# Causal attention on one core: value products two steps behind the scores and across the end of a round, copies and transposes spread over steps, masks of 128 columns

## What is computed

```python
Q = (X @ Wq.T + bq).reshape(B, S, H, d_head) * scale      # B 4, S 1024, H 16, d_head 16
K = (X @ Wk.T + bk).reshape(B, S, H, d_head) * scale
V = (X @ Wv.T + bv).reshape(B, S, H, d_head)
scores = jnp.einsum('bqhd,bkhd->bhqk', Q, K)
scores = jnp.where(causal[None, None], scores, -jnp.inf)
attn = jax.nn.softmax(scores, axis=-1)
out = jnp.einsum('bhqk,bkhd->bqhd', attn, V).reshape(B, S, D)
```

## Time and profile before

| | |
|---|---|
| median of 3 runs | 2040.08 (2039.08 to 2040.45) |
| profiled execution | 2036.14 |
| its span | 2034.0 |
| TensorE busy in the span | 1682.5 (83%) |
| VectorE, ScalarE, GpSimd busy | 1383.6, 939.3, 672.0 |
| the 15 round periods, by the first score of each | 858.34 to 1379.25 |
| last round | 1379.25 to about 1410 |

### The profile page before, as it was taken

The page is one execution under the profiler, slowest core; times in us unless marked ns, Lnnn a source line. Parts: engine busy times, 40 slices in busy tenths (PEclk is TensorE's granted clock), DMA queues, the critical chain, the costliest instruction groups (busy, mean ns, idle before and its releaser), DMA issues. The chain is left out here.

```text
span 2034.0 us, 35680 instructions
## 1 busy us (share of the span) xinstructions
PE 1682.5 (83%) x10296; PEld 1295.6 (64%) x10296; DVE 1383.6 (68%) x2825; ACT 939.3 (46%) x2201; POOL 672.0 (33%) x850
## 2 busy tenths in 40 slices
PE   2899985709991780799999999996789999979997
PEld 2787774509991560455555555542579999968886
DVE  5688887506665876977777777760467777646776
ACT  0456562304443651066666666664444444433343
POOL 1555530750007824043434334343000000047760
PEclk9799998959995995899999999998899999989999
DMA  6445523723434996333535354422774444466661
GB/s 217 181 141 168 156 47 65 230 91 117 125 113 127 332 355 190 85 105 86 147 85 144 94 129 109 118 68 64 205 216 125 125 126 125 127 212 182 202 181 47
DMA packets 288529, 293.13 MB, mean 144 GB/s; under 512 B 122665, under 2 KB 245034, under 8 KB 286300
## 3 DMA queue, kind: packets, MB, share of 16 engines
q1 hardware_dynamic: 265340, 236.62, 39.6%
q0 software_dynamic: 18432, 50.36, 7.9%
q10 hardware_dynamic: 4608, 4.20, 0.6%
HBM read 144.97 MB, written 141.82 MB: 141 GB/s over the span
## 5 line engine op out<-in xcount | busy, mean ns | idle before, releaser
L1705 ACT ACTIVATE ca_PT<-ca_psS 128x512 f32<-128x512 f32 (+3 forms) x768 | 344.9, 493 | 272.8 <-PE ca_psS L1740 260.4
L1631 DVE TENSOR_REDUCE ca_part<-ca_psM 128x1 f32<-128x512 f32 (+3 forms) x608 | 368.6, 657 | 85.3 <-PE ca_psM L1725 60.5
L1740 PE MATMUL ca_psS<-ca_QS,ca_KS 128*128 128x512 f32 (+3 forms) x768 | 305.7, 408 | 4.2 <-ACT ca_PT L1705 4.1
L1033 POOL DMA_INDIRECT g_y<-ys_scratch,pos x128 | 129.6, 1013 | 441.7 <-POOLq L68 395.0
L1718 PE MATMUL ca_psM<-ca_KS,ca_QS 126*128 126x512 f32 (+3 forms) x768 | 246.5, 364 | 15.6 <-issue 12.8
L1740 PEld LDWEIGHTS ca_psS<-ca_QS,ca_KS 128*128 128x128 f32 x768 | 147.1, 194 | 106.7 <-ACT ca_PT L1705 101.7
L1718 PEld LDWEIGHTS ca_psM<-ca_KS,ca_QS 126*128 126x128 f32 x768 | 141.1, 193 | 37.9 <-DVE ca_part L1631 15.6
L1752 PE MATMUL ca_psO<-ca_PT,ca_VA 128*32 128x512 f32 (+3 forms) x1536 | 160.7, 497 | 1.3 <-POOL ca_PT L1611 1.3
L1609 POOL TENSOR_TENSOR ca_waited<-ca_waited 1x1 f32<-1x1 f32 x128 | 23.4, 183 | 341.7 <-ACT ca_PT L1705 341.7
L626 POOL DMA_INDIRECT xs_scratch<-x_sb,pos x128 | 123.3, 964 | 36.8 <-issue 36.8
L497 PE MATMUL fa_psO<-fa_weighed,ident 128*128 128x256 f32 x512 | 124.0, 398 | 8.1 <-DVE fa_weighed L356 8.0
(11 more groups left out here) (288 smaller groups left out, 4567.2 us busy)
## 6 DMA issues: line engine op xcount, KB each, us to landing
f_xs<-xs_scratch SPq DMA_DIRECT2D x214, 128.0 KB, 2.1
ys_scratch<-f_ys SPq DMA_DIRECT2D x214, 128.0 KB, 1.7
xs_scratch<-fa_blank SPq DMA_DIRECT2D x32, 640.0 KB, 4.1
ca_QS<-qk_scratch SPq DMA_DIRECT2D x32, 512.0 KB, 6.6
ca_KS<-qk_scratch SPq DMA_DIRECT2D x32, 512.0 KB, 8.2
xs_scratch<-fa_blank SPq DMA_DIRECT2D x32, 384.0 KB, 3.4
f_raw<-in_ffn SPq DMA_DIRECT2D x16, 608.0 KB, 4.0
v_scratch<-gp_v_st SPq DMA_DIRECT2D x32, 256.0 KB, 4.5
```

What stands on the lines that cost most here:

```text
L1033: pool.indirect_dma_start(dst[:, k, :], None, y_dram, bass.IndirectOffsetOnAxis(pos[:, tile, k:k + 1], 0)).then_inc(got, 16)
L1631: dve.tensor_reduce(dst, psM[(slot * NU + u) % SLOTS][:, 0:nh * w].rearrange("p (h k) -> p h k", h=nh), AX.X, ALU.max)\
L1705: act.activation(PT[:, s % 2, h, off:CHUNK], psS[(GH * s + h) % SLOTS][:, off:CHUNK], ACT.Exp)\
L1740: pe.matmul(psS[tile % SLOTS][:, off:CHUNK], KS[:, slot, h, kt * P:(kt + 1) * P], QS[:, slot, h, c * CHUNK + off:(c + 1) * CHUNK], start=T ...
```

## The change

- `LAG` = 2: the block of step s−2 is issued at the end of step s, and this goes on over the end of a round: blocks 10 and 11 of a round stand in steps 0 and 1 of the next.
- `PT` has three buffers (`PTS`).
- `COPY`, `TURN`, `USE`: copy, transposes and division stand in steps 6, 9, 10 for c = 0, and in steps 2, 3, 4 of the next round for c = 1. On VectorE copy and division come behind the step's first unit.
- The transpose of the maxima is issued in step 7, one step behind `whole`, and the negation is split off (`negate`) into step 8.
- The mask matmul covers 128 columns a head.
- `pull` waits for the scores of the round before for Q and K and for its blocks for V; it stands ahead of the output, and the maxima rows stand ahead of the output of c = 0.
- The rows of ones are loaded in pieces of 128 elements. The rounds are written as one plain loop.

```diff
-    SLOTS = 3
+    SLOTS, PTS, LAG = 3, 3, 2
-        PT = sb("PT", [P, 2, GH, CHUNK])
+        PT = sb("PT", [P, PTS, GH, CHUNK])
-        one_rows = sb("one_rows", [2, CHUNK])
+        one_rows = sb("one_rows", [2, P])
-        ORDER = "0u1u2u3uv"
+        COPY, TURN, USE = (WHOLE - 1, 2), (WHOLE + 2, 3), (WHOLE + 3, 4)
...
-                if not (isinstance(n, int) and n < SLOTS):
-                    sp.wait_ge(oT_done, (n - SLOTS + 1) * SPAN)
+                if n >= SLOTS:
+                    sp.wait_ge(s_done, (n - SLOTS + 1) * (GH * NS))
...
+                if n >= SLOTS:
+                    sp.wait_ge(pv_done, (n - SLOTS + 1) * NS)
+                sp.dma_start(VA[:, slot, :, :], v_dram[n].rearrange("t p c -> p t c")).then_inc(stack_in[slot], 16)
...
+            for n in range(ROUNDS):
+                if n + SLOTS - 1 < ROUNDS:
+                    pull(n + SLOTS - 1)
+                if n:
+                    output(n - 1, 1)
+                if n + 1 < ROUNDS:
+                    maxima_rows(n + 1, (n + 1) % SLOTS)
                 output(n, 0)
...
         @block.vector
+            def step(n, s):
+                todo = [(n + 1 + s // WHOLE, u) for u in ahead[s] if n + 1 + s // WHOLE < ROUNDS]
+                for k in todo[:1]:
+                    unit(*k)
+                if s == COPY[1] and n:
+                    collect(n - 1, 1)
+                if s == USE[1] and n:
+                    divide(n - 1, 1)
+                if s == COPY[0]:
+                    collect(n, 0)
+                if s == USE[0]:
+                    divide(n, 0)
+                if s == WHOLE + 1 and n + 1 < ROUNDS:
+                    negate(n + 1)
+                for k in todo[1:]:
+                    unit(*k)
+                if s == WHOLE - 1 and n + 1 < ROUNDS:
+                    whole(n + 1)
...
         @block.scalar
-                    if s >= 2 or not first(n):
-                        act.wait_ge(pv_done, n * NS + s - 1)
+                    if n * NS + s >= PTS:
+                        act.wait_ge(pv_done, n * NS + s - (PTS - 1))
...
         @block.tensor
-                    m = min(w, 2 * P)
-                    mask = mask_qk[:, 2 * P - m:2 * P].unsqueeze(1).broadcast_to([P, nh, m])
-                    ins = pe.matmul(bank[:, 0:nh * w].rearrange("p (h k) -> p h k", h=nh)[:, :, w - m:w], ident_b[:, :], mask,
+                    mask = mask_qk[:, P:2 * P].unsqueeze(1).broadcast_to([P, nh, P])
+                    ins = pe.matmul(bank[:, 0:nh * w].rearrange("p (h k) -> p h k", h=nh)[:, :, w - P:w], ident_b[:, :], mask,
...
+            def step(n, s):
+                todo = [(n + 1 + s // WHOLE, u) for u in ahead[s] if n + 1 + s // WHOLE < ROUNDS]
+                for h in range(GH):
+                    scores(n, s, h)
+                    if h < len(todo):
+                        unit(*todo[h])
+                for k in todo[GH:]:
+                    unit(*k)
+                if s == TURN[1] and n:
+                    transpose_out(n - 1, 1)
+                if s == TURN[0]:
+                    transpose_out(n, 0)
+                if s == WHOLE and n + 1 < ROUNDS:
+                    transpose_maxima(n + 1)
+                if n * NS + s >= LAG:
+                    values(*divmod(n * NS + s - LAG, NS))
```

More of the change, by code:

```diff
@@ L1524, in causal_attention, with pull @@
         masked, slots_done = routing((ctx, block), PT[:, :, :, :].rearrange("p a h n -> p (a h n)"), psX)
[L1526 to L1537, removed]
         @block.sync
         def _(sp):
-            def pull(n, slot):
-                at = sp.snap(n) if not isinstance(n, int) else n
-                if not (isinstance(n, int) and n < SLOTS):
-                    sp.wait_ge(oT_done, (n - SLOTS + 1) * SPAN)
-                rows = qk_dram[:, :, bass.ds(at, 1), :, :].rearrange("c s a (r h) n -> s r c (a h n)", h=GH)
+            def pull(n):
+                slot = n % SLOTS
+                if n >= SLOTS:
+                    sp.wait_ge(s_done, (n - SLOTS + 1) * (GH * NS))
+                rows = qk_dram[:, :, n, :, :].rearrange("c s (r h) n -> s r c (h n)", h=GH)
                 for half in range(2):
@@ L1569, in _ @@
                 if n < SLOTS - 1:
[L1570 removed]
+                    pull(n)
                 if n == 0:
                     sp.wait_ge(filled, 2)
[L1573 to L1574 removed]
+                sp.dma_start(KS[STACK:P, n, :, :].rearrange("r h (c n) -> r (h c) n", n=P).bitcast(F32),
+                             one_rows[:, :].unsqueeze(1).broadcast_to([2, GH * POS_TILES, P])).then_inc(ones_done, 16)
             maxima_rows(0, 0)
[L1577 to L1582, removed]
[L1583 to L1588 removed]
+            for n in range(ROUNDS):
[5 more added lines that the diff above has]
+                    maxima_rows(n + 1, (n + 1) % SLOTS)
+                output(n, 0)
+            output(ROUNDS - 1, 1)
             for c in range(SPAN):
[L1590 removed]
                 sp.wait_ge(ao_stored[c], 16 * ROUNDS)
@@ L1636, in whole @@
                 lower, upper = part[:, 0, :, :], part[:, 1, :, TPC:]
-                if not first(n):
+                if n:
                     dve.wait_ge(mT_done, n)
@@ L1666, in divide @@
                                   ALU.mult).then_inc(o_out, 1)
-            def both(n, slot, turn, two_ahead):
-                for s in range(NS):
[L1670 to L1695, removed]
+            def step(n, s):
[16 more added lines that the diff above has]
+                    whole(n + 1)
+            for u in range(NU):
+                unit(0, u)
+            whole(0)
+            negate(0)
+            for u in range(FIRST):
+                unit(1, u)
+            for n in range(ROUNDS):
+                for s in range(NS):
+                    step(n, s)
+            collect(ROUNDS - 1, 1)
+            divide(ROUNDS - 1, 1)
         @block.scalar
@@ L1748, in values @@
                     pe.wait_ge(exp_done, n * (GH * NS) + GH * s + GH)
-                if kt == 0 and not (first(n) and c == 0):
+                if kt == 0 and (n or c):
                     pe.wait_ge(ot_out, n * SPAN + c)
@@ L1817, in _ @@
             pe.wait_ge(masked, 2)
             pe.wait_ge(ones_done, 16 * SLOTS)
-            rounds(pe, both, front, back)
+            pe.wait_ge(stack_in[0], 16 * LOADS)
+            for u in range(NU):
+                unit(0, u)
+            transpose_maxima(0)
+            pe.wait_ge(stack_in[1], 16 * LOADS)
+            for u in range(FIRST):
+                unit(1, u)
+            for n in range(ROUNDS):
+                pe.wait_ge(m_in[n % SLOTS], (n // SLOTS + 1) * 16)
+                for s in range(NS):
+                    if s == WHOLE and n + 2 < ROUNDS:
+                        pe.wait_ge(stack_in[(n + 2) % SLOTS], ((n + 2) // SLOTS + 1) * (16 * LOADS))
+                    step(n, s)
@@ L1822, in project_out @@
+            for s in range(NS - LAG, NS):
+                values(ROUNDS - 1, s)
+            transpose_out(ROUNDS - 1, 1)
 def project_out(nc, tag, o_tile, keep, s_dram, ident, wo_dram, bo_dram, scale, E, w_dram, w_hi, w_lo, shared=None):
```

120 lines of the change are left out of this document (38 added, 82 removed).

## The result

The changed kernel takes 2028.51 us (median of 6 runs, 2017.21 to 2032.23) beside 2040.07 for the kernel before (6 runs, 2034.74 to 2043.34). The ratio is 0.9938 with a 95% interval of 0.9910 to 0.9967: faster, by 7 to 18 us. Forecast was 2024, with a range of 2010 to 2034 (and a narrower one of the author's own, 2018 to 2030).

The account below looks back on a forecast made before the run. TensorE was taken to set the pace. Terms −1.29 + 0.46 + 0.62 − 0.69 = −0.90 us a round, with the end rounds −16.3 in all, gave 2024 us; range 2010 to 2034, own range 2018 to 2030.

Parts of the forecast that it names:

- the masks: Mask matmuls, 22 a round: narrower ones save 0.69 us a round, 0.10 for each of four going from 512 to 256.
- the new wait: Step 2: block 0 waits for VectorE's accumulator copy, queued behind that step's first unit; adds 0.62 us a round.
- one removed wait: Transpose of the maxima: its wait for VectorE's last maximum goes when issued one step later; −0.23 us a round.
- The removed waits: Waits at the round's end, before the maxima's transpose and at the round's start go; together −1.29 us a round.
- The end of the round: TensorE's wait for the accumulator copy before the transposes goes, with a block-to-transpose change; −0.89 us a round.
- step 0 runs into no exp: Start of the round: block 10 now stands in step 0, so ScalarE gets its time; −0.17 us a round.
- The rival of half price: Masks of 128 columns cost half, saving 0.05 each; 9.6 us more gain, 2014 us; chance 0.12.
- The separation: Blocks 10 and 11 become two blocks between scores, with one more entry and more returns; adds 0.46 us a round.
- The rounds at both ends: Round 0 gains 3.3 us, lacking earlier blocks, transposes and wait; rounds 14 and 15 together gain 1.3.
- Costed at nothing: Third value-product buffer, GpSimd's cut, SyncE's pulls, maxima rows, rows of ones and work before the first score: no cost.

Follow-up runs that it names:

- the run with 256 columns: The changed kernel with masks of up to 256 columns a head again, the new schedule kept: 2036.58 us in one run, period 34.68.
- the run with masks alone: The kernel before with masks of 128 columns and nothing else changed: 2027.86 us in one run, period 34.51.
- The pairs: The changed kernel with value blocks s-2 and s-1 together behind even steps, copies at steps 5 and 1: 2176.27 us (kernel before 2235.40); period 32.57 on a first-kind chip.
- with VectorE out of the way: The changed kernel with paired blocks, VectorE's copies and divisions first in their steps, units spread anew: 1993.28 us beside 2037.97, ratio 0.9787, period 31.8.
- the kernel with the copy first: The changed kernel with step 2's accumulator copy ahead of the step's first unit: 2018.13 us in one run, before 2040.81; period 33.50.
- the joined blocks: The changed kernel with blocks 10 and 11 together behind the next round's step 0, copy in step 1: 2172.59 us in one run, kernel before 2235.40.

## Why the prediction was right, and where its terms were off

**The stage.** Forecast −16.3, measured −12.7; the period 34.0, measured 34.23. The mechanism came as forecast, with the masks 0.24 a round too large, the new wait 0.10 too small and one removed wait 0.12 too small, so that the last two nearly cancel; that they do is luck. The median of the whole program (2028.5 against 2024) shows less than the stage does, since the stages ahead of it alone differ by 9.0 between the two profiles.

**The removed waits (−1.29)** held, and one of them was larger. The end of the round shows no idle, the maxima's transpose waits for nothing (1126.22, its block at 1126.42), and step 0 runs into no exp. But the earlier trace rows are of round 7, and round 7 is the exception for the maxima. There block 4 came 0.44 behind its score in step 5, and the transpose then waited 0.17. In the other middle rounds block 4 comes 0.32 behind, and the transpose waits 0.28. TensorE's timeline of the kernel before, steps 5 and 6 of round 8, and its waits from 858 to 1343 us:

```profile
1150.38 0.39 PE L1740 MATMUL ca_psS<-ca_QS,ca_KS 128*128 128x512 f32 x1
1150.70 1.07 PE L1752 MATMUL ca_psO<-ca_PT,ca_VA 128*32 128x512 f32 x8
...
1154.66 1.07 PE L1752 MATMUL ca_psO<-ca_PT,ca_VA 128*32 128x512 f32 x8
1156.00 0.29 PE L1733 MATMUL ca_psX<-ident,ca_maxima 128*32 128x128 f32 x1 [0.28 <-DVE ca_maxima L1641]
```

```profile
PE ca_psX L1767 <- DVE ca_OT L1656: 10.6, 13, 0.8
PE ca_psX L1733 <- DVE ca_maxima L1641: 3.6, 13, 0.3
```

Block to transpose is 1.34 there, against 1.23 in round 7 and 1.00 without a wait. So the term was −0.35 and not −0.23, another −0.12. One round read as typical was wrong by a tenth of a microsecond although the periods agree to 0.02.

**The new wait (+0.62)** was +0.72: it stands where it was placed, at the predicted instant (copy 1.27 into the step), but TensorE began 0.14 after the copy's end, and I had allowed 0.05. Moving the copy shows that the copy's place is the whole price of that wait, and that it could have been had for nothing.

**The masks (−0.69)** are the mis-sized term: −0.45 by the run with 256 columns, −0.41 by the run with masks alone. The four that went from 512 to 256 gave their 0.10 each and the one in front of a block its 0.05. The other fifteen gave nothing; I had given them 0.014 each, and two of 512 columns were left. The rival of half price is refuted by three runs: 0.45 where it wanted 1.3, 0.41 for the masks alone, and 2.66 without masks where it wanted 2.0. What holds a mask at 0.12 was not tried apart from its width; that it is the next instruction's weights stays my reading.

**The separation (+0.46)** fits the sum: −1.29 − 0.12 + 0.46 + 0.72 − 0.45 = −0.68, and 34.91 became 34.23. It is not measured apart from the removed waits; the run with 256 columns fixes only the two together. The pairs test the price of a block from the other side: six blocks fewer at 0.27 and no wait forecast 31.9, and with VectorE out of the way 31.8 came, 1.67 under the kernel with the copy first, or 0.28 a block. Loops written out, the place of the loads and the rows of ones were not tried alone; the sum leaves no room for them in a middle round.

**The rounds at both ends.** Rounds 1 to 13 gave 8.8 (forecast 11.7), the last two 1.5 (1.3). Round 0 took 32.42 instead of 34.83, 2.4 less where 3.3 was forecast. Of the missing 0.9 the period's own miss is 0.2. The rest is that without blocks in steps 0 and 1 its units outrun VectorE. TensorE's timeline in step 2 of round 0, then the weight loads of its two units:

```profile
871.62 0.50 PE L1708 MATMUL ca_psM<-ca_KS,ca_QS 126*128 126x512 f32 x1
871.96 0.28 PE L1727 MATMUL ca_psS<-ca_QS,ca_KS 128*128 128x256 f32 x1
872.22 0.50 PE L1708 MATMUL ca_psM<-ca_KS,ca_QS 126*128 126x512 f32 x1
...
871.62 0.19 PEld L1708 LDWEIGHTS ca_psM<-ca_KS,ca_QS 126*128 126x128 f32 x1 [0.16 <-DVE ca_part L1617]
872.22 0.19 PEld L1708 LDWEIGHTS ca_psM<-ca_KS,ca_QS 126*128 126x128 f32 x1 [0.22 <-DVE ca_part L1617]
```

Unit to score is 0.34 where 0.23 is the price, and score to unit 0.26 where it is 0.12. It is the same backlog that spoiled the joined blocks, and I had costed it at nothing.

**Costed at nothing, and so:** the maxima rows' load is issued at 1131.39, 8.1 before the round that needs it; nine were forecast. Cuts and scatters hold nobody. Block 4 in step 6 does not wait.

**Open:** what the waits in steps 6 to 8 are on the other chips, and why the change gains 2.5% there. The kernel before was not profiled on such a chip, so where that gain lies was not seen. The profile of the changed kernel there shows where the waits begin. It is on ScalarE and VectorE, not on TensorE. Step 6 of round 6, three of its lines:

```profile
1122.02 0.50 PE L1727 MATMUL ca_psS<-ca_QS,ca_KS 128*128 128x512 f32 x1
...
1123.79 0.60 ACT L1694 ACTIVATE ca_PT<-ca_psS 128x512 f32<-128x512 f32 x1 [1.29 <-PE ca_psO L1739]
...
1124.46 0.69 DVE L1617 TENSOR_REDUCE ca_part<-ca_psM 128x1 f32<-128x512 f32 x1 [1.97 <-PE ca_psM L1712]
```

The first exp starts 1.77 after its score, where 0.6 is usual, and the reduction 1.6 after the end of its unit's mask (1122.82). The next exps start 1.4 apart. Each instruction takes as long as on the first chips (0.60 and 0.69); only the starts are late. The cause was not found. The round is not where most of the difference lies either: of the 152 us between the two profiles of the changed kernel (2182.84 and 2031.21), 21 lie ahead of the first score, 39 in the stage and 92 behind it.

## What to carry to other kernels

Where one engine is fed without gaps, count distances from start to start, not busy time: a shorter mask was busy 0.05 less and saved nothing, while each block of column-strip value products put by itself between full-array scores cost 0.27, so that putting them in pairs (−1.67 together with VectorE's work respread) was worth more than all the lag (−0.23, or −0.96 with the copy first). Read several rounds before calling one typical. When a wait is moved into the next round, look at what the released work now queues behind on the helping engine: here one reduction ahead of a copy gave back 0.72 of the 0.89 that the move had won. Taking a long block out of a stretch also takes away the time in which the helping engine catches up; spread its work before joining blocks.

## What the runs showed of the hardware

A mask matmul of 128 columns and one of 256 take the same 0.12 on the path between matmuls of units and scores; one of 512 takes 0.22. And the kernel before took 2040 us on some chips and 2214 to 2235 on others. TensorE's granted clock over the span was 0.92 to 0.93 of full speed on the first and 0.89 to 0.90 on the others, but in a middle round of the changed kernel it is 1.00 on both, and most steps of a round are equal to the hundredth. The difference sits in certain stretches, and so the gain of a schedule was 2.5% on one chip (interval 1.8 to 3.2) and 0.6% on another (0.3 to 0.9).
